# One transfer of 6 KB runs instead of three of 2 KB runs for the weights of each of 64 experts

## The chip, the cores and the metric

The kernel runs on one core of one Trainium2 chip, alone. The metric is the device time of one execution in microseconds (us), lower is better. Three runs of the kernel before are given, and one profiled execution.

## The reference, cut to what matters

A two-layer gated block on `x` (4 x 512 x 512, float32): attention with a mixture of 8 experts behind it, then a summary attention with a second mixture of 64 experts. All arithmetic here is float32. The change touches the weights of the last mixture:

```python
flat = x.reshape(N, Dx)                    # N = 2048 tokens of 512
scores = jax.nn.softmax(flat @ Wr + router_bias, axis=-1)
topk_scores, topk_idx = jax.lax.top_k(scores, 4)
...
xb = jnp.zeros((64, 128, Dx)).at[eid, pos].set(flat[tok], mode='drop')
h = jax.nn.silu(jnp.einsum('ecd,edh->ech', xb, Wg)) * jnp.einsum('ecd,edh->ech', xb, Wu)
yb = jnp.einsum('ech,ehd->ecd', h, Wd)     # Wg, Wu: 64 x 512 x 128, Wd: 64 x 128 x 512
out = ...                                  # each token's 4 rows of yb, weighted, and shared experts
```

Each of the three weights of an expert has 65536 float32, 256 KB.

## The kernel before, in words

The program has stages, one after the other, each a block of instruction lists for the five engines with a barrier behind it.

- `attention` (first layer, with routing of the first mixture) and `summary_and_tiles`.
- `mixture0`: the first mixture, 40 tiles of 128 sorted rows.
- `middle`: gathers the first mixture's results, adds the summary attention, routes the tokens to the 64 experts, computes three quarters of the shared experts, and scatters the normalised tokens into the HBM table `tab1`, 128 rows for each expert. GpSimd issues the scatters (L1238).
- `experts`: the 64 experts, one per step.
- `finish`: gathers four result rows for each token from `ytab1` (L1748, GpSimd), adds them up on VectorE (L1774), computes the last quarter of the shared experts, stores the output.

The expert loop is software-pipelined. In step i TensorE transposes the tokens of expert i + 1 (L1648, four 128 x 128 blocks), computes both up-projections of expert i (L1656, 16 matmuls) and the down-projection of expert i - 1 (L1662). ScalarE copies the transposed tokens (L1677) and takes the silu (L1681); VectorE multiplies (L1704) and copies the result out of PSUM (L1708) to a ring of four tiles, from which it is stored.

All transfers of the loop are issued by SyncE, in this order in step i, the first two as soon as the down-projection of expert i - 1 is done (semaphore `y_full`), the last as soon as VectorE has copied its result:

- the tokens of expert i + 3, 256 KB from `tab1`, rows of 2 KB, to a ring of four tiles `m_x` (L1624);
- the weights of expert i + 7, by `load_expert`: three transfers of 256 KB (L1579);
- the store of the result of expert i - 1, 256 KB to `ytab1` (L1633).

The weights go to a ring of eight slots (`expert_slot`, L1560), each of three times 2 KB in each of the 128 partitions, lying directly behind one another; six slots lie in tiles that the routing stage no longer uses (in the profile `y`, `stage_up`, `stage_gate`), two in a tile of their own (`m_w`). Weight k of expert e is read as 128 runs of 2 KB: partition p takes row group p, `"(p b) h -> p (b h)"`. So the experts 0 to 4 (`W_EARLY`) can be loaded before the loop: `middle` issues them on SyncE as their slots come free (L1213 to L1216). Each slot has one semaphore, which the weights and the tokens that belong to the same expert raise by 16 for each transfer. TensorE waits for it before the transposes (L1645):

```python
need(pe, loaded[(q + 1) % W_RING], (u + (q + 1) // W_RING) * 64 + 64)
```

that is 64 for every expert in this slot: three weights and the tokens.

Of the kernel before, what the change touches and what calls it, by code (L numbers as in the profile page):

```python
# [5 lines left out]
F32 = mybir.dt.float32  # L6
# [8 lines left out]
P = 128  # L15
B, SEQ, D = 4, 512, 512
# [5 lines left out]
E1, H1, TOP1, CAP1 = 64, 128, 4, 128  # L22
# [7 lines left out]
W_RING = 8  # L30
# [9 lines left out]
def need(eng, sem, value, alone=0):  # L40


    if not isinstance(value, int):
        if alone:
            eng.wait_ge(sem, alone)
        eng.wait_ge(sem, value)
    elif value > 0:
        eng.wait_ge(sem, value)
# [9 lines left out]
def valid(*tiles, n=TILES):  # L58
    return all(not isinstance(k, int) or 0 <= k < n for k in tiles)


def steps(eng, step, n, ring, lead, tail):

    first, last = max(-(-lead // ring), -(-4 // ring)), (n - lead) // ring
    for i in range(-lead, first * ring):
        step(i, i // ring, i % ring)
    with eng.Fori(first, last) as u:
        for c in range(ring):  # L70
            step(u * ring + c, u, c)
    for i in range(last * ring, n + tail):
        step(i, i // ring, i % ring)
# [1016 lines left out]
def middle(nc, A, T):  # L1090
# [4 lines left out]
    with c:  # L1095
# [99 lines left out]
        @block.sync  # L1195
        def _(sp):
            sp.dma_start(gamma[:], A["L1_xattn_gamma"].partition_broadcast(P)).then_inc(small_loaded, 16)
            sp.dma_start(beta[:], A["L1_xattn_beta"].partition_broadcast(P)).then_inc(small_loaded, 16)
            sp.dma_start(wr[:], A["L1_ffn_Wr"].rearrange("(b p) e -> p b e", p=P)).then_inc(small_loaded, 16)
            sp.dma_start(bias_r[:], A["L1_ffn_router_bias"].partition_broadcast(P)).then_inc(small_loaded, 16)  # L1200

            sp.wait_ge(gathered[TPB - 1], 16 * 2)
            for s in range(NSH):
                sp.dma_start(stage[0][:, s].rearrange("p (b h) -> p b h", b=DB),
                             A["L1_ffn_Sg"][s].rearrange("(b p) h -> p b h", p=P)).then_inc(gate_loaded, 16)
            for s in range(NSH):
                sp.dma_start(T["w_sd"][:, s], A["L1_ffn_Sd"][s].rearrange("(b p) h -> p b h", p=P)).then_inc(sd_loaded, 16)

            free = {0: ((x2_ready, TILES),), 2: ((lg_full, TILES), (fT_kept, TILES)),
                    3: ((shared.y_full, groups_done * TPB),)}
            for e in range(W_EARLY):  # L1213
                for used, count in free.get(e, ()):
                    sp.wait_ge(used, count)
                load_expert(sp, A, T, e, e)  # L1216
# [343 lines left out]
def expert_slot(T, n):  # L1560

    if n in (5, 6):
        return T["w1"][:, n - 5]
    t, at = {0: ("y0", 0), 1: ("y0", 3), 2: ("stage_up", 0), 3: ("stage_gate", 0), 4: ("stage_gate", 3),
             7: ("stage_up", DB)}[n]
    t = T[t][:]
    t = t.rearrange("p j k d -> p (j k) d") if len(t.shape) == 4 else t.rearrange("p s (b h) -> p (s b) h", h=D)
    return t[:, at:at + 3, :]


def load_expert(sp, A, T, n, e):

    slot = expert_slot(T, n)
    for k, name in enumerate(("L1_ffn_Wg", "L1_ffn_Wu", "L1_ffn_Wd")):
        if isinstance(e, int):
            w = A[name][e].rearrange("(p b) h -> p (b h)", p=P)
        else:
            w = A[name][bass.ds(e, 1)].rearrange("o (p b) h -> p (o b h)", p=P)
        sp.dma_start(slot[:, k, :], w).then_inc(T["s_w1"][n], 16)  # L1579


def experts(nc, A, T):
# [4 lines left out]
    with c:  # L1587
# [10 lines left out]
        loaded = T["s_w1"]  # L1598
# [7 lines left out]
        g, h = spare[:, 0:2], spare[:, 2:4]  # L1606
# [10 lines left out]
        @block.sync  # L1617
        def _(sp):
            def step(i, u, q):

                e = i + AHEAD
                if valid(e, n=E1):
                    need(sp, y_full, i)
                    sp.dma_start(xb[:, (q + AHEAD) % RING, :],  # L1624
                                 T["tab1"][bass.ds(e * CAP1, CAP1), :]).then_inc(loaded[(q + AHEAD) % W_RING], 16)
                e = i + W_RING - 1
                if valid(e, n=E1) and (not isinstance(e, int) or e >= W_EARLY):
                    need(sp, y_full, i)
                    load_expert(sp, A, T, (q - 1) % W_RING, e)
                if valid(i - 1, n=E1):  # L1630
                    n = (q - 1) % RING
                    need(sp, y_ready, i)
                    sp.dma_start(T["ytab1"][bass.ds((i - 1) * CAP1, CAP1), :], y[:, n, :]).then_inc(stored[n], 16)  # L1633

            steps(sp, step, E1, W_RING, W_RING - 1, 1)
            for s in range(RING):
                sp.wait_ge(stored[s], 16 * E1 // RING)

        @block.tensor
        def _(pe):  # L1640
            def step(i, u, q):
                s, o = q % 2, 1 - q % 2
                if valid(i + 1, n=E1):
                    n = (q + 1) % RING
                    need(pe, loaded[(q + 1) % W_RING], (u + (q + 1) // W_RING) * 64 + 64)  # L1645
                    need(pe, xT_ready, i)
                    for b in range(DB):
                        last = nc.tensor.transpose(pX[o][:, b * P:b * P + P],  # L1648
                                                   xb[:, n, :].rearrange("t (p b) -> t b p", b=DB)[:, b, :], ident[:])
                    last.then_inc(xT_full, 1)  # L1650
                if valid(i, n=E1):
                    need(pe, xT_ready, i + 1)
                    need(pe, h_ready, i - 1)
                    for k, w in enumerate(up_w[q]):
                        for b in range(DB):
                            last = nc.tensor.matmul(pH[s][:, k * CAP1:(k + 1) * CAP1], w[:, b, :], xT[:, s, b, :],  # L1656
                                                    start=(b == 0), stop=(b == DB - 1))
                    last.then_inc(h_full, 1)
                if valid(i - 1, n=E1):
                    need(pe, h_ready, i)  # L1660
                    need(pe, y_ready, i - 2)
                    nc.tensor.matmul(pY[o][:], h[:, o, :], slots[(q - 1) % W_RING][:, 2, :],  # L1662
                                     start=True, stop=True).then_inc(y_full, 1)

            steps(pe, step, E1, W_RING, 1, 1)
# [120 lines left out]
class SharedExperts:  # L1786
# [61 lines left out]
INPUTS = (  # L1848
    "x", "ctx_2048", "g_xattn", "g_ffn", "L0_ffn_w_gate", "L0_ffn_wi_0", "L0_ffn_wi_1", "L0_ffn_wo",
    "L1_xattn_decay", "L1_xattn_W_in", "L1_xattn_b_in", "L1_xattn_W_out", "L1_xattn_b_out",  # L1850
    "L1_xattn_gamma", "L1_xattn_beta", "L1_ffn_Wr", "L1_ffn_router_bias", "L1_ffn_Wg", "L1_ffn_Wu",
    "L1_ffn_Wd", "L1_ffn_Sg", "L1_ffn_Su", "L1_ffn_Sd")


# [18 lines left out]
```

## Time and profile before

| | |
|---|---|
| median of three runs | 1309.43 us |
| runs | 1305.15 to 1312.16 us |
| span of the profiled execution | 1295.4 us |
| TensorE / weight load busy | 1076.8 (83%) / 745.9 us (58%) |
| VectorE / ScalarE / GpSimd busy | 786.8 (61%) / 487.2 (38%) / 573.3 us (44%) |
| transfers | 112637 packets, 210.19 MB, mean 162 GB/s |

The span reaches from the first to the last instruction of one execution; the time of a run also holds what lies before and behind it, so the span is read against itself and the difference of 14.0 us to the median is launch and end. A separate time of the profiled execution is not given; its span is 9.8 us under the fastest run. A line of the profile names the source line, the engine and `out<-in`; `SPq` is the queue of SyncE. The DMA share is the mean busy share of the 16 transfer engines of the core; `q1` is the queue of the transfers that SyncE issues, `q0` that of GpSimd's, `q14` and `q8` fetch instructions. The queue rows give packets, MB, and the time that the packets took as a share of 16 engines.

### The profile page before, as it was taken

To read this page: it belongs to the slowest core of one execution; us is meant where nothing else is said; L and a number is where in the kernel's file an instruction comes from. 1 tells how busy PE (TensorE), PEld (TensorE's weight loads), DVE (VectorE), ACT (ScalarE), POOL (GpSimd) and SP (SyncE) were. 2 spreads that over 40 slices of the span, in tenths; PEclk is the share of its full clock that TensorE was granted. 3 is DMA by queue.
4 is the path that set the end of the run, shared out by engine and by line. 5 is a ranking of instruction groups with operands and counts; after the bars stand their busy time and mean duration, and the time that the engine had idled before them with its cause. 6 is when DMAs were issued, how large, how long until landed. Compare 5 with 4: busy or idle time off the path is not lost. (4 is left out here: it accounts for less than half of the span.)

```text
span 1295.4 us, 20041 instructions
## 1 busy us (share of the span) xinstructions
PE 1076.8 (83%) x5303; PEld 745.9 (58%) x5303; DVE 786.8 (61%) x1897; ACT 487.2 (38%) x855; POOL 573.3 (44%) x734
## 2 busy tenths in 40 slices
PE   3998999999859999997078999989068898888984
PEld 2555555555256777776066575675056666666751
DVE  4678788787227888885878678586312222222565
ACT  2456555555217888884231211112022222221000
POOL 6366555564335676665816344462400000000775
PEclk9999999999958999997589999999579999999997
DMA  9554334541443333324411120220379999995776
GB/s 314 190 163 155 118 119 146 177 162 66 157 148 134 106 106 105 107 96 138 147 51 60 34 85 24 73 73 4 113 249 332 332 340 339 343 332 205 212 238 200
DMA packets 112637, 210.19 MB, mean 162 GB/s; under 512 B 16073, under 2 KB 24265, under 8 KB 112578
## 3 DMA queue, kind: packets, MB, share of 16 engines
q1 hardware_dynamic: 96578, 166.42, 38.0%
q0 software_dynamic: 16000, 43.13, 10.4%
q8 instruction: 19, 0.31, 0.1%
q14 instruction: 40, 0.33, 0.1%
HBM read 141.22 MB, written 77.59 MB: 169 GB/s over the span
## 5 line engine op out<-in xcount | busy, mean ns | idle before, releaser
L1748 POOL DMA_INDIRECT y<-ytab,take x64 | 68.9, 1076 | 281.5 <-POOLq L1587 262.3
L965 POOL TENSOR_TENSOR m_down_lo<-wo,m_down_hi 128x512 fp32r<-128x512 f32 x80 | 133.2, 1685 | 80.4 <-ACT m_down_hi L1040 80.4
L476 PE MATMUL bank<-win,vT 128*128 128x512 f32 x256 | 124.6, 600 | 0.0
L1704 DVE TENSOR_TENSOR stage_gate<-stage_gate,bank 128x128 f32<-128x128 f32 x64 | 18.4, 287 | 166.2 <-ACT stage_gate L1681 166.2
L1813 PE MATMUL bank<-flat_hi,w_hi 128*128 128x512 f32 x256 | 103.5, 404 | 13.3 <-DVE stage_gate L1826 5.2
L646 DVE TENSOR_REDUCE negmax<-bank 128x1 bf16<-128x512 f32 x128 | 86.9, 679 | 40.8 <-PE bank L483 40.5
L569 ACT ACTIVATE win<-bank 128x512 f32<-128x512 f32 x128 | 69.4, 594 | 100.3 <-PE bank L468 99.8
L1054 DVE TENSOR_TENSOR m_up_lo<-w,m_up_hi 128x1024 fp32r<-128x1024 f32 x80 | 99.2, 1241 | 10.2 <-ACT m_up_hi L1027 8.3
L1813 PE MATMUL bank<-flat_hi,w_lo 128*128 128x512 f32 x256 | 101.1, 395 | 0.0
L1813 PE MATMUL bank<-flat_lo,w_hi 128*128 128x512 f32 x256 | 100.8, 394 | 0.0
L1238 POOL DMA_INDIRECT tab<-stage_up,slot x64 | 67.0, 1048 | 73.9 <-DVE slot L1455 57.2
L1648 PE MATMUL bank<-ident,m_x 128*128 128x128 f32 x256 | 47.6, 310 | 61.8 <-DMA m_x<-tab 61.4
L1648 PEld LDWEIGHTS bank<-ident,m_x 128*128 128x128 f32 x256 | 36.6, 209 | 107.6 <-DMA m_x<-tab 98.6
L483 PE MATMUL bank<-k_hi,q_parts 128*128 128x512 f32 x128 | 71.4, 557 | 22.2 <-DVE q_parts L724 13.1
L1836 PE MATMUL bank<-w_sd,stage_gate 128*128 128x512 f32 x192 | 84.2, 594 | 4.1 <-DVE stage_gate L1826 4.1
L1677 ACT COPY y<-bank 128x512 f32<-128x512 f32 x64 | 37.5, 585 | 110.1 <-PE bank L1648 110.1
L1774 DVE SCALAR_TENSOR_TENSOR x_sb<-y,wt,x_sb 128x512 f32<-128x512 f32 x64 | 48.2, 753 | 42.5 <-DMA y<-ytab,take 38.9
L986 PE MATMUL bank<-m_up_hi,m_xT_hi 128*128 128x512 f32 x160 | 70.6, 441 | 3.2 <-DVE m_up_lo L1054 3.2
L483 PEld LDWEIGHTS bank<-k_hi,q_parts 128*128 128x128 f32 x128 | 25.1, 196 | 74.9 <-DVE negmax L646 43.8
L1813 PEld LDWEIGHTS bank<-flat_hi,w_hi 128*128 128x128 f32 x256 | 48.9, 191 | 26.6 <-DVE stage_gate L1826 7.1
L986 PE MATMUL bank<-m_up_lo,m_xT_hi 128*128 128x512 f32 x160 | 63.9, 399 | 0.0
L986 PE MATMUL bank<-m_up_hi,m_xT_lo 128*128 128x512 f32 x160 | 63.8, 399 | 0.0
(271 smaller groups left out, 2598.4 us busy)
## 6 DMA issues: line engine op xcount, KB each, us to landing
m_x<-tab SPq DMA_DIRECT2D x104, 256.0 KB, 3.2
tab<-zeros SPq DMA_DIRECT2D x16, 1024.0 KB, 10.9
ytab<-summary SPq DMA_DIRECT2D x64, 256.0 KB, 5.2
ytab<-m_y SPq DMA_DIRECT2D x40, 256.0 KB, 2.0
wout<-in_ctx SPq DMA_DIRECT2D x64, 128.0 KB, 2.6
w<-in_L_ffn_wi SPq DMA_DIRECT2D x16, 512.0 KB, 5.6
wo<-in_L_ffn_wo SPq DMA_DIRECT2D x8, 512.0 KB, 7.2
wout<-in_ctx SPq DMA_DIRECT2D x16, 256.0 KB, 2.9
```

The costliest lines, as they stand in the source:

```text
L476: nc.tensor.matmul(pO[s * 2 + h][:], vT[:, s, sb_, h:h + 2, :].rearrange("p a c -> p (a c)"), probs[:, sb_ % 2, h, :], start=(sb_ == 0), s ...
L483: nc.tensor.matmul(pM[:], q_parts[:, s, h, t * P:t * P + P], k_hi[:, s, h, :], start=True, stop=True).then_inc(pm_full, 1)
L569: nc.scalar.activation(probs[:, b % 2, h, :], pS[h][:], ACT.Exp, scale=1.0 / HEAD).then_inc(p_ready, 1)
L646: nc.vector.tensor_reduce(negmax[:, s, m:m + 1], pM[:], AX.X, ALU.max, negate=True).then_inc(pm_read, 1)
L965: nc.gpsimd.tensor_tensor(dn_lo[:, m, :], row(wo0, e * MB + m), dn_hi[:, m, :], ALU.subtract).then_inc(dn_lo_ready, 1)
L986: last = nc.tensor.matmul(pH[s][:], x[:, s, d, :], w[:, d, :], start=(d == 0 and part == 0), stop=(d == DB - 1 and part == 2))
L1054: nc.vector.tensor_tensor(up_lo[:, at, :], blocks(w01, e * DB + half * HALF, HALF), up_hi[:, at, :], ALU.subtract).then_inc(up_lo_ready, 1)
L1238: nc.gpsimd.indirect_dma_start(T["tab1"], bass.IndirectOffsetOnAxis(slot1[:, j, k:k + 1], 0), flat[:, j, :], None, bounds_check=E1 * CAP1 ...
L1648: last = nc.tensor.transpose(pX[o][:, b * P:b * P + P], xb[:, n, :].rearrange("t (p b) -> t b p", b=DB)[:, b, :], ident[:])
L1748: nc.gpsimd.indirect_dma_start(y1[:, t % RING, k, :], None, T["ytab1"], bass.IndirectOffsetOnAxis(take1[:, t, k:k + 1], 0)).then_inc(gathe ...
L1813: last = nc.tensor.matmul(bank[:], w[:, k, s, cols], x[:, d, :], start=(d == 0 and part == 0), stop=(d == DB - 1 and part == 2))
L1836: last = nc.tensor.matmul(pY[j][:], self.h[:, n, j * P:j * P + P], sd[:, s, b, :], start=(n == 0), stop=(n == self.CHUNKS - 1))
```

## The change

The three weights of an expert are laid side by side in one input `expert_weights` (64 x 128 x 1536), made on the host before the launch: row p of expert e holds the 2 KB run of partition p of `Wg`, then that of `Wu`, then that of `Wd`. The three inputs of before are no longer given to the device. `load_expert` issues one transfer of 768 KB, 128 runs of 6 KB on both sides; the bytes arrive at the same places as before. The semaphore of a slot rises by 32 for each expert, not 64, and TensorE's wait is changed to that.

```diff
 def load_expert(sp, A, T, n, e):
 
-    slot = expert_slot(T, n)
-    for k, name in enumerate(("L1_ffn_Wg", "L1_ffn_Wu", "L1_ffn_Wd")):
-        if isinstance(e, int):
-            w = A[name][e].rearrange("(p b) h -> p (b h)", p=P)
-        else:
-            w = A[name][bass.ds(e, 1)].rearrange("o (p b) h -> p (o b h)", p=P)
-        sp.dma_start(slot[:, k, :], w).then_inc(T["s_w1"][n], 16)
+    slot = expert_slot(T, n).rearrange("p k d -> p (k d)")
+    w = A["expert_weights"][e] if isinstance(e, int) else \
+        A["expert_weights"][bass.ds(e, 1)].rearrange("o p w -> p (o w)")
+    sp.dma_start(slot, w).then_inc(T["s_w1"][n], 16)
...
-                    need(pe, loaded[(q + 1) % W_RING], (u + (q + 1) // W_RING) * 64 + 64)
+                    need(pe, loaded[(q + 1) % W_RING], (u + (q + 1) // W_RING) * 32 + 32)
...
+    packed = np.concatenate([np.asarray(inputs[name]).reshape(E1, P, D) for name in PACKED], axis=2)
+    arrays["in_expert_weights"] = np.ascontiguousarray(packed)
```

## Rows read from the trace of the kernel before

**Rows 1.** The page's 40 slices of 32.4 us: DMA share in tenths, and rate.

```profile
DMA  9554334541443333324411120220379999995776
GB/s 314 190 163 155 118 119 146 177 162 66 157 148 134 106 106 105 107 96 138 147 51 60 34 85 24 73 73 4 113 249 332 332 340 339 343 332 205 212 238 200
```

**Rows 2.** Busy time by stretch; the first line names the columns.

```profile
core 0: us, PE busy (x) PEld busy (x) DVE busy (x) ACT busy (x) POOL busy (x), PEclk, DMA share, GB/s
...
963.00:1170.00 207.00, 176.93 (x1166) 136.15 (x1166) 51.65 (x107) 45.71 (x106) 0.00 (x0) 1.00 0.98 336
1170.00:1197.00 27.00, 23.08 (x152) 18.11 (x152) 8.18 (x16) 5.45 (x13) 0.00 (x0) 1.00 0.56 198
1197.00:1295.00 98.00, 75.01 (x256) 50.15 (x256) 55.61 (x76) 4.78 (x8) 68.89 (x64) 0.89 0.71 215
```

**Rows 3.** Timeline of TensorE, 1050 to 1062 us: start, duration, line, tiles, count.

```profile
1053.33 0.75 PE L1648 MATMUL bank<-ident,m_x 128*128 128x128 f32 x4
...
1055.71 1.03 PE L1662 MATMUL bank<-stage_up,stage_gate 128*128 128x512 f32 x2
1058.07 0.75 PE L1648 MATMUL bank<-ident,m_x 128*128 128x128 f32 x4 [1.34 <-DMA m_x<-tab]
```

**Rows 4.** Timeline of SyncE's queue, 1050 to 1062 us, the same columns.

```profile
1053.69 0.33 SPq L1624 DMA_DIRECT2D m_x<-tab  x1
1054.21 0.35 SPq L1579 DMA_DIRECT2D y<-in_L_ffn_Wg  x1
...
1055.71 0.36 SPq L1633 DMA_DIRECT2D ytab<-summary  x1
1056.92 0.33 SPq L1624 DMA_DIRECT2D m_x<-tab  x1
...
1061.66 0.33 SPq L1624 DMA_DIRECT2D m_x<-tab  x1
```

**Rows 5.** Waits, 963 to 1170 us: total us, times, longest us.

```profile
PEld bank L1648 <- DMA m_x<-tab: 63.0, 47, 2.9
...
SPq L1624 <- PE bank L1662: 69.3, 54, 2.9
```

**Rows 6.** Tile m_x, 963 to 1170 us: its loads, min/median/max us to landing.

```profile
L1624 SPq DMA_DIRECT2D m_x<-tab x54: 327/333/443, 962.7 to 1169.8; - x54
...
DMA to landing us min/median/max: 2.8/4.3/5.2
```

**Rows 7.** DMA, 963 to 1170 us: slices, packets, queue share of 16 engines, issues.

```profile
GB/s 372 333 328 358 316 328 319 341 305 363 342 351 305 317 347 325 367 343 341 333 342 350 321 371 295 365 329 353 320 325 352 333 369 297 359 286 376 321 346 318
DMA packets 38226, 69.66 MB, mean 336 GB/s; under 512 B 4247, under 2 KB 4247, under 8 KB 38222
...
q1 hardware_dynamic: 38222, 69.60, 98.1%
...
stage_gate<-in_L_ffn_Wd SPq DMA_DIRECT2D x14, 256.0 KB, 5.1
```

**Rows 8.** DMA, 592.8 to 594.3 us: one store in 2 KB packets, engines else idle.

```profile
q1 hardware_dynamic: 144, 0.26, 45.2%
```

**Rows 9.** DMA, 676 to 679.5 us: two rows of 2 KB in one 4 KB packet.

```profile
DMA packets 160, 0.52 MB, mean 150 GB/s; under 512 B 32, under 2 KB 32, under 8 KB 160
...
q0 software_dynamic: 160, 0.52, 36.7%
```

**Rows 10.** DMA, 1001 to 1003 us: the stretch with one 8 KB instruction fetch.

```profile
q14 instruction: 1, 0.01, 1.0%
```

**Rows 11.** DMA, 907 to 917 us: nine weight loads and nothing else.

```profile
q1 hardware_dynamic: 1296, 2.36, 69.2%
```

**Rows 12.** DMA, 640 to 650 us: gathers in packets of 4 KB.

```profile
q0 software_dynamic: 493, 1.63, 58.7%
```

**Rows 13.** The page's DMA queues, whole span.

```profile
q1 hardware_dynamic: 96578, 166.42, 38.0%
```

More of the change, by code:

```diff
@@ L1850 @@
     "L1_xattn_decay", "L1_xattn_W_in", "L1_xattn_b_in", "L1_xattn_W_out", "L1_xattn_b_out",
-    "L1_xattn_gamma", "L1_xattn_beta", "L1_ffn_Wr", "L1_ffn_router_bias", "L1_ffn_Wg", "L1_ffn_Wu",
-    "L1_ffn_Wd", "L1_ffn_Sg", "L1_ffn_Su", "L1_ffn_Sd")
+    "L1_xattn_gamma", "L1_xattn_beta", "L1_ffn_Wr", "L1_ffn_router_bias", "L1_ffn_Sg", "L1_ffn_Su", "L1_ffn_Sd")
+PACKED = ("L1_ffn_Wg", "L1_ffn_Wu", "L1_ffn_Wd")
 def kernel(**inputs):
@@ L1868 @@
         A[name] = nc.dram_tensor(f"in_{name}", a.shape, mybir.dt.from_np(a.dtype), kind="ExternalInput").ap()
+    packed = np.concatenate([np.asarray(inputs[name]).reshape(E1, P, D) for name in PACKED], axis=2)
+    arrays["in_expert_weights"] = np.ascontiguousarray(packed)
+    A["expert_weights"] = nc.dram_tensor("in_expert_weights", packed.shape, F32, kind="ExternalInput").ap()
     out = nc.dram_tensor("out", inputs["x"].shape, mybir.dt.float32, kind="ExternalOutput").ap()
```

## The prediction

> **What bounds the kernel now.** I read the 40 slices first: only from slice 30 to slice 36 does the DMA share stay at 9 tenths, at 332 to 343 GB/s [rows 1]. Cut into stretches, that is the expert loop: from 963 to 1170 us the 16 DMA engines are busy 98% of the time, the matmuls 85% at a full clock, the vector, scalar and GpSimd engines 25% or less; in the 27 us behind it, when the last weights are in, the DMA share falls to 0.56, and the gathers of the last stage have a different limit [rows 2]. Then I asked who waits. TensorE's transposes wait for the load of `m_x`, an expert's tokens: 63.0 us on its weight loads, and SyncE waits only for the matmul whose count lets it refill buffers, 69.3 us; it isn't short of issue time [rows 5]. The timelines show the pattern: one step (one expert) passes in 3.23 us when nothing is late (SyncE's token issues at 1053.69 and 1056.92), the next in 4.74 (1056.92 to 1061.66), because the transposes stood still until 1058.07 [rows 3, 4]. So TensorE's own pace is 3.23 us a step. Between the first and the last of the 54 token loads of this stretch lie 53 steps and 207.1 us, **3.91 us a step** [rows 6].
>
> Why is the load late? It is asked for one step before its transposes, and lands 4.3 us later in the median, 2.8 at best [rows 6]: it queues behind the weights and the store of the step before. The queue's packets fill 98.1% of 16 engines for 207 us with 38222 packets, 4247 of them the small ones with which a transfer reports, 16 for each [rows 7]. That is 3249 us of engine time, 3.83 us a step and engine. The transfer engines set the pace, the others have slack; a packet's price decides what the change is worth.
>
> **The price of a packet.** One store that ran alone has 128 packets of 2 KB and 16 small ones in 45.2% of 16 x 1.5 us, 10.8 us: 84 ns a packet [rows 8]. The 128 packets of 4 KB of the scatter took 36.7% of 16 x 3.5 us, 20.6 us with 32 small ones: 158 ns [rows 9]. A line through both has 37 ns a KB and 9 or 10 ns that don't depend on size; with the latter I price the small packets, 9 ns. The one instruction fetch of 8 KB took 1.0% of 32 us, 0.32 us; the line gives 0.31 [rows 10]. So one packet of 6 KB costs 84 + 2 x 75 = **234 ns** where three of 2 KB cost 252.
>
> In the loop a step has five transfers (three weights, tokens, store) of 8 packets an engine: 40 x 84 + 5 x 9 = 3.405 us. Measured are 3.83. The missing 0.43 us, 10.7 ns a packet, are stalls: the rate per slice swings between 286 and 376 GB/s [rows 7], while 84 ns a packet would give 390. They come with loads alone too: nine weight transfers without a store, 1152 packets, took 69.2% of 160 us, 95 ns each [rows 11].
>
> **The change, part by part.**
> - Three weight transfers become one: per engine 24 packets of 84 ns become 8 of 234, 2.016 to 1.872 us, saving 0.144.
> - Two reports of 9 ns go: 0.018. Together 0.162 us; a step's work without stalls is 3.243.
> - The stalls: if they go by bytes, they stay at 0.43 and the step saves 0.162. If they go by packets, 16 of 40 are gone, 16 x 10.7 = 0.171 more, so 0.333. Rows for a contended 6 KB packet don't exist; the ends are these, and I take the middle, 0.25, since 2 KB packets alone can't tell them apart.
> - Steps that profit: 54, those of the stretch with full engines. The seven steps behind it load no weights; the weights of experts 0 to 4 come during the routing stage, before they are needed. Sum: 54 x 0.162 = 8.7 us at the low end, 54 x 0.333 = 18.0 at the high end, 13.4 in the middle. The step would then be 3.5 to 3.7 us, still above TensorE's 3.23, so transfers stay the bound and the whole gain reaches the end; from nearness to that floor (random lateness that TensorE can't make up) I take 1 us off: **12.4 us**.
> - SyncE's queue: two issues of 0.33 to 0.38 us a step go [rows 4], so the store behind them can be issued up to 0.9 us earlier. It is not waited for soon and the order of the ring stays tokens, weights, store. SyncE is idle 69.3 us there [rows 5], so this is worth nothing by itself; without that cover it would be up to 0.9 us a step. If transfers became fast, TensorE's 3.23 us would be the next bound.
> - The wait for 32 instead of 64 falls at the same event, the last of weights and tokens. Nothing is moved past another queue's work: GpSimd issues nothing in this loop. The same bytes land at the same places.
> - Slots in the routing stage: nine of its 15 weight transfers are the burst of rows 11; it ends long before the loop. No gain, no loss.
>
> A check of the price with the Trainium skill. The row shows 9 ns of cost apart from size [rows 8, 9]. The page "DMA: Bandwidth & Descriptors", section "Why small descriptors are slow (HBM only)", speaks of about 3 cycles of overhead per packet on the internal bus, on a fabric of 850 MHz, which would be an estimated 3.5 ns. By that, 16 packets less save 0.06 us a step and the low end would be 4 us, too little to be measured; the trace's line is 2.5 times that, and the sum goes by it.
>
> All this is a difference. The profiled span is 1295.4 us; the median of the three runs, 1309.43, is 14.0 above it (launch and end, which the change doesn't touch; the runs reach from 1305.15 to 1312.16). 1309.4 - 12.4 = **1297.0 us**.
>
> **The rivals.**
> 1. *The packets don't get larger, or their size is worth little* (0.19). If the queue cuts a 6 KB run at 2 KB, only two reports of 9 ns go: 54 x 0.018 = 1 us, 1308. Cut at 4 KB it is 16 packets, 8 x (158 + 84): 0.07 + 0.018 + up to 8 x 10.7 ns, 5 to 9 us, 1300 to 1304. For it: SyncE's queue has no packet above 2 KB in this program, so nothing shows that it makes one. Against: the instruction queue carries 8 KB packets at the line's price [rows 10].
> 2. *Large packets stall more: slower* (0.14). The place is the weight packet in the loop, the price its stall, the turning point 52 ns a packet of 6 KB (the 32 that three stall now plus the 20 saved). The gathers from HBM in 4 KB packets took 58.7% of 160 us for 1.63 MB, about 398 packets of 236 ns [rows 12], 78 more than the undisturbed 158; in proportion a 6 KB packet would stall 117, 65 over the point, 0.52 us a step: 28 us, 1337. At half of that excess it is 1323. For: nothing else above 2 KB was measured under load. Against: those are scattered rows, the weights are one contiguous block, and streaming 2 KB packets stall only 11.
> 3. *The fixed part of a transfer counts* (0.05). A token load needs 2.8 us at best [rows 6], of which 8 packets are 0.67; if the other 2.1 were paid in turn, dropping two transfers would put the step on TensorE's 3.23 us: 54 x 0.68 = 37 us, 1273. Against it: the packets alone fill 98.1% of the engines [rows 7], so these parts run beside each other. The Trainium skill has this rule on the same page, under "Rules for kernel authors": small transfers are to be coalesced, at least 1 MiB for the full rate; the trace bears it out only for transfers that nobody overlaps.
>
> **How the numbers follow.** The forecast's case (0.62) lies between 1289 and 1301. A change of 0.5%, 6.5 us, is about what a measurement of this kernel can tell from none. Faster: 0.60 of the forecast's case (its rest falls within 0.5%) and rival 3, 0.65. Same: rival 1, the 0.02 and a mild form of rival 2, 0.22. Slower: 0.13. The range goes from 1283 (the forecast with stalls of the weights gone altogether, 54 x 0.42 = 23 us, and the spread of the runs) to 1315 (no change, and that spread); it leaves out rival 3 and the strong form of rival 2, under 2 in 10.
>
> **What would show it.** Right: SyncE's queue falls from 96578 packets by 64 x (256 + 32) to some 78100 [rows 13]; a count with packets "under 8 KB" alone can't tell 2 from 6, but the packet count does. The steps of the loop take 3.6 to 3.75 us between token issues; the DMA share stays at 0.96 or more and the rate rises to 350 to 365 GB/s; the token load lands in about 4 us; the stages before 945 us and from the last matmul of the loop to the end take what they took. Wrong: a packet count near 94500 (rival 1), the loop's rate at or under 336 GB/s at full share with fewer packets (rival 2), or a share well under 0.95 with steps of 3.25 us (rival 3).

## The result: slower by 0.6%, and the profile after

Over 20 runs of each kernel the change takes 1314.01 us in the median against 1305.18, a ratio of 1.0063 with a 95% interval from 1.0045 to 1.0081. It is slower by a little more than can be told from no change. Forecast were 1297.0 us and a gain.

The runs also correct a reading of the prediction. A profiled run's own time is given with the later results, and it is 1.7 us above its span (1319.3 and 1317.6 us for the profile below). So the profile of before, with its span of 1295.4 us, belongs to an execution of about 1297 us, 8 us faster than the median, and not to one with 14 us of launch and end. The spans of the two profiles differ by 22 us, the medians by 9: the rest is the scatter of executions.

The page's slices of the kernel after, which answer to [rows 1], and its queue of SyncE, which answers to [rows 13]:

```profile
DMA  9544433441543333326310210311288999985676
GB/s 316 180 160 160 135 117 130 159 159 65 176 147 118 106 109 104 104 94 196 99 52 37 65 44 23 99 48 74 72 307 288 311 330 326 334 287 204 205 235 207
...
q1 hardware_dynamic: 78146, 166.41, 37.4%
```

The packets were merged as the edit says: 78146, the number forecast. The rate in the loop fell.

The same stretch of the loop in the kernel after, 963 to 1193 us, in the views of [rows 2, 5, 6, 7]: the token loads with min/median/max us to landing, the busy times with granted clock, DMA share and GB/s, the packets, and the waits (total us, times, longest).

```profile
L1621 SPq DMA_DIRECT2D m_x<-tab x55: 327/333/346, 965.3 to 1192.5; - x55
...
DMA to landing us min/median/max: 2.7/4.6/6.8
```

```profile
963.00:1193.00 230.00, 189.80 (x1204) 146.91 (x1203) 53.55 (x110) 47.20 (x110) 0.00 (x0) 0.96 0.90 313
```

```profile
DMA packets 23675, 71.93 MB, mean 313 GB/s; under 512 B 2625, under 2 KB 2625, under 8 KB 23672
...
q1 hardware_dynamic: 23672, 71.89, 89.9%
```

```profile
PEld bank L1645 <- DMA m_x<-tab: 71.9, 47, 4.5
```

Between 55 token loads lie 54 steps and 227.2 us: 4.21 us a step, 3.91 before. The engines' share is 0.90, not 0.98. Their work per step and engine fell, from 0.981 x 3.91 = 3.83 us to 0.899 x 4.21 = 3.78, and yet the step got longer. A token load takes up to 6.8 us to land, before 5.2 at most. So the transfer engines did not set the pace.

One of the long steps, in the timeline of TensorE (start, duration, line, tiles, idle before):

```profile
1152.00 1.95 PE L1653 MATMUL bank<-y 128*128 128x128 f32 x16
1153.79 1.02 PE L1659 MATMUL bank<-stage_up,stage_gate 128*128 128x512 f32 x2
1158.50 1.13 PE L1645 MATMUL bank<-ident,m_x 128*128 128x128 f32 x4 [3.69 <-DMA m_x<-tab]
1159.42 3.62 PE L1653 MATMUL bank<-y 128*128 128x128 f32 x16
1162.83 1.74 PE L1659 MATMUL bank<-y,stage_gate 128*128 128x512 f32 x2
1164.41 0.63 PE L1645 MATMUL bank<-ident,m_x 128*128 128x128 f32 x4
```

and the two stretches around it (the last three columns are granted clock, DMA share, GB/s):

```profile
1153.00:1158.00 5.00, 1.81 (x11) 0.98 (x9) 0.98 (x2) 0.28 (x1) 0.00 (x0) 0.94 1.00 333
1158.00:1165.00 7.00, 6.50 (x28) 5.49 (x29) 0.58 (x2) 0.86 (x2) 0.00 (x0) 0.55 0.42 158
```

TensorE idles 3.69 us for tokens, and the clock granted behind that is mostly the lower of its two levels, 1.2 GHz (0.55 of full on average): the 16 matmuls of L1653 take 3.62 us where they took 1.95 one step earlier. Meanwhile nobody asks for transfers, and the DMA share falls to 0.42. A late token load thus costs its wait and can cost half a step more. Over the loop the granted clock is 0.96, before it was 1.00 [rows 2]: TensorE spent 17 us of the change's loop at 1.2 GHz and none of the loop before.

This is not a small part. Of a step of 3.91 us before, TensorE was busy for 176.93/207, 3.34 us, and idle for 0.57; of a step of 4.21 in the change it was busy for 189.80/230, 3.47 us, and idle for 0.74. So of the 0.30 us that a step of this profile is longer, about 0.17 are waiting and about 0.13 the lower clock.

### The profile page after: what moved, and what is told of

The parts are those of the page before. It is cut to its first block and busy times, and to the rows that moved or that the text cites. A ratio compares the mean times of both kernels' runs of the same rounds, so it can differ in the third digit from the quotient of the medians.

```text
span 1317.6 us, 19817 instructions
## 1 busy us (share of the span) xinstructions
PE 1082.7 (82%) x5303; PEld 750.6 (57%) x5303; DVE 787.0 (60%) x1897; ACT 487.5 (37%) x855; POOL 574.5 (44%) x734
## 3 DMA queue, kind: packets, MB, share of 16 engines
q1 hardware_dynamic: 78146, 166.41, 37.4%
```

## The experiments

Each run is compared with the kernel before on its own chip; ratios are to that, with 95% intervals. "Step" is the time between token issues in its profile.

### Packet size, one transfer, or the place in HBM

**The change again** (no edit):

> The changed kernel again, so that the others of this call can be compared with it on the same chip, and a second profile of it. Both theories: ratio to before 1.005 to 1.008, about 1314 us against 1305. The profile shows whether the long steps of the expert loop (over 6.5 us between two token loads: 5 of them in the first profile of the change, none in that of before) and the DMA share of 0.89 come back. If they were an accident of one execution, the loop takes 239 us from the first token issue to the last as before, not 257.

Measured: 1.009 [1.0057, 1.0123], 1315.96 us. Step 4.19 us, share 0.91, tokens landing up to 6.9 us: no accident.

**One transfer in runs of 2 KB:**

```diff
-    slot = expert_slot(T, n).rearrange("p k d -> p (k d)")
-    w = A["expert_weights"][e] ...
-    sp.dma_start(slot, w).then_inc(T["s_w1"][n], 16)
+    w = A["expert_weights"][e].rearrange("k p w -> p k w") ...
+    sp.dma_start(expert_slot(T, n), w).then_inc(T["s_w1"][n], 16)
...
+    packed = np.stack([... .reshape(E1, P, D) for name in PACKED], axis=1)
```

> One transfer of 768 KB for each expert, but in runs of 2 KB: 384 packets of 84 ns instead of 128 of 234. Theory A, the size of the packets is to blame (a packet of 6 KB stalls 47 ns beyond its 234 where three of 2 KB stall 32, and the stalls are on single engines, so that tokens land late on one of them): the ratio to before is 0.998 to 1.001, the loop as before. Theory B, the single transfer is to blame (weights and store are issued 0.9 us earlier and stand in front of the next tokens as one block): the ratio is that of the change, 1.005 to 1.008, with long steps.

Measured: 1.0038 [1.0023, 1.0054], 1309.08 us; step 4.05 us. Neither theory alone: it lies between, clear of both no change and the change on the same chip. About 0.4% comes with the single transfer and 0.5% more with the larger packets. The second pair of this kind, further down, has 1.0036 and 1.0075.

**Three transfers of 2 KB runs from the packed input:**

```diff
+    for k in range(3):
+        sp.dma_start(slot[:, k, :], w[:, k * D:(k + 1) * D]).then_inc(T["s_w1"][n], 16)
```

> The packed input, each expert still loaded by three transfers of 2 KB runs, which now lie 6 KB apart in HBM. Theory A (packet size) and theory B (one transfer): as before, ratio 0.998 to 1.001. Theory C, the new place of the bytes in HBM is to blame (runs 6 KB apart): the ratio is that of the change, 1.005 or more, with packets of 2 KB that stall more than 10.7 ns in the mean.

Measured: 0.9996 [0.9983, 1.001]; step 3.95 us. The new place of the bytes costs nothing.

### Tokens asked for earlier

At the moment of step i at which the tokens of expert i + 3 are asked for, the transposes of expert i + 1 are already done, so two of the four buffers are free. The edit uses them; it leaves nothing out.

```diff
-        AHEAD = RING - 1
+        AHEAD = RING + 1
...
                     need(sp, y_full, i)
+                    if isinstance(i, int):
+                        need(sp, xT_full, i + AHEAD - RING + 1)
                     sp.dma_start(xb[:, (q + AHEAD) % RING, :],
```

> The change with the tokens of expert i + 5 instead of i + 3 asked for in step i (the same four buffers, of which two are free by then). Theory A and B alike say that the transfer engines have less work than before (3.70 us a step against 3.83, DMA share 0.89) and that the loss is the wait for tokens that land late on one engine: with tokens asked for three steps ahead the share goes to 0.97 or more, the step to 3.75 us and the ratio to 0.988 to 0.994 (about 1293 us). The rival, that large packets take so much more engine time that the transfers themselves are slower: the ratio stays above 1.003.

Measured: **0.9614** [0.9597, 0.9632], 1252.7 us against 1303.2. Far beyond the expectation, whose direction held and whose size (1293 us) did not. The token loads, 960 to 1124 us, the busy times, and the DMA slices, packets and share in the middle of the loop, 975 to 1110 us:

```profile
L1623 SPq DMA_DIRECT2D m_x<-tab x52: 327/333/347, 962.6 to 1121.7; - x52
...
DMA to landing us min/median/max: 6.3/8.1/8.8
```

```profile
960.00:1124.00 164.00, 164.00 (x1161) 139.27 (x1160) 51.16 (x105) 45.64 (x106) 0.00 (x0) 1.00 1.03 413
```

```profile
GB/s 399 405 415 417 418 418 411 422 419 418 416 415 417 417 415 415 417 420 419 419 417 418 417 418 416 416 415 417 417 416 418 418 418 418 420 419 418 417 415 417
DMA packets 18484, 56.20 MB, mean 416 GB/s; under 512 B 2050, under 2 KB 2050, under 8 KB 18482
...
q1 hardware_dynamic: 18482, 56.17, 103.1%
```

A step takes 159.1 / 51 = 3.12 us and TensorE is never idle. The slices swung from 286 to 376 GB/s [rows 7]; now nearly all stand at 415 to 420. What I had read as stalls is gone, though the same bytes come from the same places faster: by the trace a 6 KB packet takes 234.5 ns in the mean here and 281 in the change (985 to 1190 us). The stalls of the other kernels are rare and long: 96 in 100 of the 2 KB packets in the loop before took their 84 ns, and the few others up to 1.8 us. (The share passes 1 because records of neighbouring packets on one engine overlap a little.) The Trainium skill gives the rule on its page "DMA: Bandwidth & Descriptors", under "Rules for kernel authors": issue early, wait late, and the fixed part overlaps. This trace agrees: a token load now takes 8.1 us to land, and TensorE's weight loads wait for it for 4.2 us in all, before for 63.0 [rows 5].

**The same edit on the kernel before:**

> The kernel before (three transfers, 2 KB) with the tokens of expert i + 5 asked for in step i. The last call's run of the change with this edit had no stalls at all: packets of 84.1 and 234.5 ns in the mean, engines full at 1.03, step 3.12 us. Theory D: what looked like stalls are engines whose queue had run dry, so they go here too; with deep queues only the undisturbed price counts, 3.41 us a step over 1.03, 3.30 us, against the 3.12 of the packed one, 0.18 x 54 = 10 us: about 1262 us, ratio 0.967 to 0.971, packets of 84 to 85 ns. The rival, that 2 KB packets stall by themselves (memory): packets stay at 94 ns, the step at 3.75 to 3.83 us, ratio 0.990 to 0.995.

Measured: 0.963 [0.96, 0.9661], 1264.69 us. Here too the stalls went, 84.0 ns a packet. The size was near the forecast one, but not for its reason: the step is 3.17 us and not 3.30, at 406 GB/s; the chips differ (the kernel before took 1313 us on this one and 1303 on that of the run above), which makes most of the distance to 1252.7.

**One transfer of 2 KB runs with it:**

> One transfer of 2 KB runs for each expert, tokens two steps earlier. With deep queues the moment at which a transfer is issued should count for nothing, only its packets: two reports of 9 ns less than with three transfers, 1 us. Theory D: within 3 us of the run with three transfers (about 1261 us), and 8 to 10 us above the change with earlier tokens (1252.7). If one transfer of 768 KB is bad in itself, it is 5 us above the run with three, as it was without the earlier tokens.

Measured: 0.9629 [0.9598, 0.966], 1263.84 us, within 1 us of three transfers. With early tokens a single transfer costs nothing. The expected 8 to 10 us above 1252.7 compared different chips; the two runs below settle that.

**The change with tokens one step earlier** (`AHEAD = RING`):

> The change with the tokens of expert i + 4 asked for in step i, one step earlier and not two. In the change a token load lands after 4.4 us in the median and 6.8 at most, and is needed one step (3.2 us) after it is asked for; one step more makes that 6.4 us, enough for nearly all. Theory D, lateness of tokens is the whole loss: ratio 0.96 to 0.975, 1252 to 1270 us, hardly a wait of TensorE. If the transfer engines are the bound by work or stalls, one step more doesn't change the rate: ratio above 0.995.

Measured: 0.9622 [0.9589, 0.9654], 1262.41 us. Its loads land in 5.8 us, at most 6.6, and TensorE still waits a little:

```profile
L1623 SPq DMA_DIRECT2D m_x<-tab x53: 327/333/347, 957.1 to 1121.8; - x53
...
DMA to landing us min/median/max: 4.9/5.8/6.6
```

```profile
PEld bank L1647 <- DMA m_x<-tab: 23.2, 41, 1.3
PE bank L1647 <- DMA m_x<-tab: 0.8, 2, 0.5
```

One step of lead is nearly all of it: 3.17 us a step. Lateness of tokens, with the clock that falls behind it, is the loss of the loop, in the change and before.

**Both kernels with early tokens, on one chip:**

> Three transfers of 2 KB with the tokens two steps earlier, beside its packed counterpart on one chip (the two ran on different chips so far: ratios to before 0.963 and 0.9614). Both are at TensorE's own pace, 3.12 to 3.17 us a step, so the packets hardly count: ratio 0.960 to 0.966.

> The change with the tokens two steps earlier, beside the run above. If packets of 6 KB are worth anything once nobody waits for tokens, it is 1 to 4 us faster than three transfers of 2 KB with the same edit (0.02 to 0.05 us a step); 9 us or more would mean that the predicted price of a packet reaches the end; slower would mean that large packets hurt with deep queues too.

Measured: 0.966 [0.9633, 0.9688] and 0.9636 [0.9611, 0.966], 1264.43 and 1263.20 us. The intervals overlap; if the packets are worth anything it is 1 to 3 us. The views of [rows 6] for the two, three transfers first:

```profile
L1626 SPq DMA_DIRECT2D m_x<-tab x52: 327/333/898, 960.7 to 1122.4; - x52
...
DMA to landing us min/median/max: 5.2/8.6/9.3
```

```profile
L1623 SPq DMA_DIRECT2D m_x<-tab x52: 327/333/347, 962.3 to 1121.4; - x52
...
DMA to landing us min/median/max: 6.1/7.2/7.9
```

161.7 / 51 = 3.17 and 159.1 / 51 = 3.12 us a step. The packed kernel is at TensorE's own pace, which is 3.12 and not the 3.23 that I had read from steps of the kernel before. The one with three transfers is so only at first. Its waits and its transfers, 960 to 1124 us:

```profile
PEld bank L1650 <- DMA m_x<-tab: 13.9, 23, 0.7
```

```profile
DMA packets 36388, 66.30 MB, mean 404 GB/s; under 512 B 4042, under 2 KB 4042, under 8 KB 36385
```

Up to 1050 us it also takes 3.12 us a step, but at a steady 406 GB/s its loads land later and later, after 6.5 us at 980 and 9.3 at 1064. From then on the tokens are late again, and from 1080 us a step takes 3.22 us, about what the 1.31 MB of a step need at 406 GB/s (an estimate, 3.23). So in this stretch the transfer engines do set the pace. The packed kernel moves 417 GB/s and its loads slip from 6.9 to 8.0 us by the end of the loop, too little to be waited for: it has no wait for tokens in this stretch. In a longer loop the size of the packets would be worth more than it was over 64 experts; no run shows by how much.

### What makes the tokens later in the change

A transfer runs on 16 engines and has landed when the last has reported; the Trainium skill says so on the page "DMA: Bandwidth & Descriptors", under "Why a DMA increments its semaphore by 16 and not by 1". The trace has all 16 reports. I took those of the token loads between 980 and 1125 us, from the issue, in us: the first engine, the middle one and the last, each as its median over the loads, and for the last also what 1 load in 10 exceeds.

```
kernel                        first   middle   last   last, 1 in 10
before                         2.55     3.13   4.33            4.80
one transfer, 2 KB             2.75     3.00   4.02            5.59
the change                     2.45     2.87   4.56            5.74
change, weights issued last    3.52     3.99   4.90            5.81
```

The tokens are needed 3.1 to 3.2 us after the issue, or later when TensorE had to wait in the step between. Half of the engines deliver in time in all of the first three kernels, in the change soonest; the last one comes 1.2 us late before and 1.4 after, and the worst tenth is 0.9 us later than before. With one transfer of 2 KB runs only the worst tenth is later (0.8 us); its median is earlier. The packets became cheaper on average and the slowest engine slower.

**The change with the weights issued last** (the blocks of weights and store exchanged in SyncE's step):

> The change with the order tokens, store, weights in each step: the weights are issued 1 us later, behind VectorE's copy. Theory D, a queue that runs dry between the store of one step and the tokens of the next costs more than its idle time: the packets' work ends about 1 us later in the step, the gap before the next tokens is shorter, and the ratio falls from the change's 1.007 to 0.995 to 1.002. The rival, theory B, a block of 768 KB standing in front of the next tokens delays them: now it stands directly before them, so the ratio is the change's or worse, 1.007 to 1.02.

Measured: 1.0172 [1.0126, 1.0218], 1336.46 us; step 4.36 us, clock 0.93 over the loop. My theory of dry queues (D) forecast the opposite and falls; the rival holds: weights that stand directly in front of the tokens delay all engines by about 1 us (middle 3.99). A part of the 1.7% is the clock: 0.07 of the loop's 230 us are 16 us of TensorE time at most, of 23 us.

**The same exchange in the kernel before:**

> The kernel before with the order tokens, store, weights: the same three transfers of 2 KB, now directly in front of the next tokens. The same edit made the change 1.0 to 1.7% slower than the change itself. Theory E: it is what stands in front of the tokens at the slowest engine, so this kernel loses too, ratio 1.005 to 1.015. If that loss belongs to packets of 6 KB, the ratio is 0.998 to 1.002.

Measured: 1.0021 [0.9986, 1.0057]. Inconclusive: the loss, if there is one, is less than expected, a fraction of that of the single block of 768 KB. Its profile has a step of 4.04 us and tokens up to 5.8 us to land, between before and the change.

**Three transfers of 6 KB runs**, split by partitions:

```diff
+    for p, q in ((0, 48), (48, 96), (96, 128)):
+        sp.dma_start(slot[p:q], w[p:q]).then_inc(T["s_w1"][n], 16)
```

> The packed weights in runs of 6 KB, but again three transfers for each expert, of 48, 48 and 32 partitions: the fourth corner beside three of 2 KB (ratio 0.9996 from the packed input), one of 2 KB (1.0038) and one of 6 KB (1.0063 and 1.009). Theory E: the loop waits for the slowest of the 16 engines that bring the tokens, and both parts of the change make that engine later, larger packets (a longer piece in front of the tokens) and the single transfer (all weights in the ring 0.9 us earlier), each by about 5 us: ratio 1.002 to 1.006. If the size of the packets alone is harmless and only the single transfer counts, it is 0.998 to 1.001; if the two parts don't add up, it is the change's, 1.006 to 1.009.

Measured: 1.0387 [1.0357, 1.0418], 1361.53 us. This was meant to be the fourth corner and is not: the split brought a cost of its own. DMA of this kernel, 1040 to 1140 us:

```profile
DMA packets 10094, 28.51 MB, mean 285 GB/s; under 512 B 1743, under 2 KB 1743, under 8 KB 10094
...
q1 hardware_dynamic: 10094, 28.51, 103.5%
```

Engines full, and only 285 GB/s: 1.26 times the engine time for a byte that the change has (0.90 at 313). By the trace a 6 KB packet takes 394 ns in the mean (985 to 1190 us), and not by a few long ones: the median is 387, in the change 234. So it tells nothing about the two parts of the change.

**The moment of the store.** With one transfer, SyncE issues the store 0.9 us earlier. Two tiny transfers in front of it bring back most of that (by the profiles 1.8 and 1.7 us behind the tokens, 2.0 before, 1.0 to 1.1 without them), once with one transfer of 2 KB runs, once in the change:

```diff
+                    for k in range(2):
+                        sp.dma_start(scratch[0:1, 2 * n + k:2 * n + k + 1], A["L1_xattn_decay"]).then_inc(stored[n], 16)
                     sp.dma_start(T["ytab1"]...
```

> One transfer of 2 KB runs, and in front of the store two tiny transfers of 4 bytes, so that the store is issued 2.0 us after the tokens as in the kernel before and not 1.1 us. If the earlier store is what costs the 0.4% of the single transfer, the ratio falls from 1.0038 to 0.999 to 1.002. If not (the weights as one piece cost it, or a tiny transfer has its own price in front of the next tokens), it is 1.003 to 1.008.

> The change with the same two tiny transfers in front of the store. If the moment of the store counts, about 0.4% below the change of this call: ratio 1.001 to 1.005. If it doesn't: the ratio of e15, 1.006 to 1.009, or a little above.

Measured: 1.0036 [1.0017, 1.0055] and 1.0075 [1.0045, 1.0105]. Without them 1.0038 (another chip) and 1.0067. Nothing came back, so the earlier store is probably not the cost; a price of the tiny transfers that just hides a gain is not ruled out.

**Two transfers, runs of 4 KB and 2 KB:**

```diff
+    for c in (0, 2 * D):
+        at = slice(c, min(c + 2 * D, 3 * D))
+        sp.dma_start(slot[:, at], w[:, at]).then_inc(T["s_w1"][n], 16)
```

> Two transfers for each expert, one of 512 KB in runs of 4 KB (gate and up weights) and one of 256 KB in runs of 2 KB. Between three of 2 KB (0.9996) and one of 6 KB (1.006 to 1.009) in both respects; if both cost in proportion, the ratio is 1.002 to 1.006; if the whole cost comes only with the single transfer or with more than 4 KB, 0.999 to 1.001.

Measured: 1.0018 [0.9994, 1.0041]: between the ends, but not clear of no change.

**The change once more, on that chip:**

> The change on the chip of this call: ratio 1.006 to 1.010; its profile has steps of over 6 us in the expert loop and a DMA share of 0.89 to 0.93 there.

Measured: 1.0067 [1.0037, 1.0098], 1322.20 us; step 4.15 us, share 0.90, as expected.

## Why the prediction was wrong

- **What bounds the kernel: the step that failed.** The prediction had "the transfer engines set the pace, the others have slack", from the 98.1% of [rows 7]. The busy time of a transfer engine contains what its packets wait: 0.43 us a step of it were stalls, seen and counted by the prediction as work. They are a consequence: with tokens asked for earlier the same kernel moves 406 GB/s at 84 ns a packet. The bound was the loop from "down-projection done" over token issue and landing to the transposes, with one step, 3.1 to 3.2 us, to do it in, and 4.3 us needed [rows 6]. The prediction had that row and the sentence "asked for one step before its transposes", and took the lateness as a symptom of full engines. One test of arithmetic was at hand: a load that lands after 4.3 us is 1.1 us late for a step of 3.2. The wait gives the next load that much more time, so a long step follows a short one, as 4.74 us follow 3.23 in [rows 4], and the mean of two steps is (3.2 + 4.3) / 2, an estimate of 3.75 us. That is most of the way from 3.2 to the measured 3.91, without any limit of bandwidth.
- **The price of a packet: right.** 234 ns forecast, 234 measured as the undisturbed value and 234.5 as the mean with early tokens. By the Trainium skill's page "DMA: Bandwidth & Descriptors", under "Why small descriptors are slow (HBM only)", the overhead is an estimated 3.5 ns a packet, which would give 3 x 84 - 2 x 3.5 = 245; this trace has 9 ns and 234. It was the right price of a thing that nobody waited for. With early tokens the lower price shows as 417 GB/s against 406, but only the second half of the loop with 2 KB packets waits for it; TensorE's 3.12 us hide the rest, and in place of 0.16 us a step, 9 us, the two kernels are 1.2 us apart.
- **The stalls: mis-sized, and in the wrong sum.** Put between "by packets" and "by bytes", 0.26 to 0.43 us a step. A 6 KB packet takes 281 ns in the loop, a stall of 47 where three of 2 KB have 32: more than by bytes. With 0.13 us for the other 16 packets it is 0.5 us. That is rival 2, just under its turning point of 52 ns, so the work of the engines fell slightly; the loss came from which engine stalls, not from the sum.
- **SyncE's queue: worth nothing.** The runs with the store nearly at its old moment agree, as far as they can tell.
- **The packed place and the count of packets: right** (0.9996; 78146).
- **TensorE's pace of 3.23 us: 3.12.** And its clock was taken as granted: it fell to 1.2 GHz in the loop of the change, 17 us in all and worth some 0.13 us of the profile's 0.30 us a step, which the prediction did not price.
- **The baseline.** The 14 us between span and median were launch and end only for 1.7; the rest was the scatter of executions.
- **The rivals.** The slower one had the right sign, at 0.13, and the right place (a stall of the large packets) but a mechanism of total work, with 1323 to 1337 us. In rival 1 the cut at 4 KB saves 0.08 us and not 0.07, which changes nothing. Missing was the rival that happened: the closed loop of the tokens.

What is shown: tokens that land late are the loss, in both kernels; one transfer and larger packets each make it worse, by about 0.4 and 0.5%; the place in HBM does not. Not shown is how much of those 0.4 and 0.5% is wait and how much the clock that falls behind waits, what stalls a single engine for one or two us while queues are short and hardly ever when they are long, and by which way a single transfer with the same packets makes the worst tenth of the loads later. Three transfers of 6 KB packets without a split by partitions were not tried.

## What to carry to other kernels

A transfer queue that is busy 98% of the time need not be the limit: look at the rate in its slices, and if it swings below what the undisturbed packets would give, ask first how early the load that somebody waits for is issued. Here one constant (and a wait in the first steps), tokens asked for two steps earlier into buffers that were free anyway, brought 3.4 to 3.9%, six times what the change cost, and left the size of the packets worth about 1 us. Only then was the queue near its limit, and the sign was another: a steady rate, and loads that land a little later in each step. Before merging transfers in a tight loop, see what stands behind them in the queue: the small load that is needed next has landed only when the slowest of 16 engines has brought its share. And see whether longer waits bring TensorE's clock down, which costs on top of them.

## What the runs showed that I had not expected

- Stalls inside packets vanish with long queues: 6 KB packets 281 ns in the mean with loads landing in 4.6 us, 234.5 with 8.1; 2 KB packets 94.5 and 84.
- The first and the last of the 16 engines of one 256 KB load report 1.5 us apart before and 1.8 in the change, in the median of the loads between 980 and 1125 us.
- Transfers of 48, 48 and 32 partitions take 1.26 times the engine time per byte of one with 128, 394 ns for a 6 KB packet. The Trainium skill advises against splitting by partitions, on the page "DMA: Bandwidth & Descriptors" under "Rules for kernel authors", since the parts would serialize; here it was worse than that.
- TensorE's clock fell to 1.2 GHz in the middle of a busy loop, in four places of the change's: three lie behind idle stretches of 2.5, 2.8 and 3.7 us, the fourth behind one of 1.9. In the loop before, with idle stretches of up to 2.1 us, it did not fall.
